# Attention in eight places of the array, a step that spans three pairs, and x folded into W0, in a fused four-layer kernel

## The reference

```python
x = x + _L0_cond_ref(x, W, A, Bm, scalings, idx0)  # x W^T + rank-16 adapter of 8: (x A_b^T) B_b^T s_b
x = x + _L1_cond_ref(x, idx1, w1)                  # einsum('bct,bcd->bdt'): mixes the 64 tokens, 1 of 200 matrices
x = x + _L2_cond_ref(x, cond, Wq, Wk, Wv, Wo)      # causal attention, 16 heads of 32, q scaled by min(cond, 4)
x = x + _L3_cond_ref(x, idx3, w3)                  # as layer 1, 1 of 8 matrices
```

## Time and profile before

| | |
|---|---|
| median of 3 runs | 714.54 us (713.11 to 714.82) |
| profiled execution | 714.74 us, span 713.2 us |
| mean granted TensorE clock | 0.988 |
| TensorE matmul rows | 683.2 us busy, 96% of the span |
| TensorE weight loads | 584.7 us, 82% |
| VectorE, ScalarE, GpSimd | 378.9, 319.9, 113.9 us |
| DMA | 31.68 MB, 44 GB/s over the span |

### The profile page before, as it was taken

The page is one execution under the profiler, slowest core; times in us unless marked ns, Lnnn a source line. Parts: engine busy times, 40 slices in busy tenths (PEclk is TensorE's granted clock), DMA queues, the critical chain, the costliest instruction groups (busy, mean ns, idle before and its releaser), DMA issues.

```text
span 713.2 us, 14872 instructions
## 1 busy us (share of the span) xinstructions
PE 683.2 (96%) x5240; PEld 584.7 (82%) x5240; DVE 378.9 (53%) x565; ACT 319.9 (45%) x648; POOL 113.9 (16%) x98
## 2 busy tenths in 40 slices
PE   5699999999999999999999999999999999999986
PEld 4489797888979798797979879797987979798774
DVE  3645555464555646455564645546463554636362
ACT  3544355443535544353554435354543535444342
POOL 4003012030301203030120303002030300303030
PEclk9979999999999999999999999999999999999998
DMA  6520111102011010201101020110202011020000
GB/s 185 191 94 8 53 37 35 49 4 81 7 52 37 33 52 4 81 7 52 37 30 54 5 81 7 52 37 18 65 5 81 7 52 37 9 75 4 29 1 30
DMA packets 32768, 31.68 MB, mean 44 GB/s; under 512 B 18550, under 2 KB 18550, under 8 KB 32758
## 3 DMA queue, kind: packets, MB, share of 16 engines
q1 hardware_dynamic: 32758, 31.55, 14.2%
HBM read 22.61 MB, written 8.91 MB: 44 GB/s over the span
## 4 chain that ended last, share of the span: by engine, by line
PE 92%; DMA 2%; DVE 2%; SPq 1%; issue 1%; ACT 0%; POOL 0%; ACTq 0%; DVEq 0%
PE banks L374 13%; PE banks L375 12%; PE banks L376 12%; PE banks L504 9%; PE banks L472 8%; PE banks L493 5%; PE banks L421 5%; PE banks L512 4%; PE banks L481 4%; PE banks L404 4%; PE banks L402 4%; PE banks L406 4%; PE banks L436 2%; PE banks L395 2%; PE banks L385 2%; PE banks L414 2%
## 5 line engine op out<-in xcount | busy, mean ns | idle before, releaser
L374 PE MATMUL banks<-x1T_hi,w_hi 128*128 128x256 f32 x512 | 148.3, 290 | 0.0
L375 PE MATMUL banks<-x1T_lo,w_hi 128*128 128x256 f32 x512 | 144.9, 283 | 0.0
L376 PE MATMUL banks<-x1T_hi,w_lo 128*128 128x256 f32 x512 | 144.8, 283 | 0.0
L374 PEld LDWEIGHTS banks<-x1T_hi,w_hi 128*128 128x128 f32 x512 | 98.1, 192 | 15.3 <-issue 15.3
L375 PEld LDWEIGHTS banks<-x1T_lo,w_hi 128*128 128x128 f32 x512 | 98.1, 192 | 0.0
L376 PEld LDWEIGHTS banks<-x1T_hi,w_lo 128*128 128x128 f32 x512 | 98.0, 191 | 0.0
L742 DVE COPY k_bd<-banks 32x512 f32<-32x512 f32 x64 | 44.2, 691 | 98.9 <-PE banks L376 98.2
L907 POOL TENSOR_TENSOR w_own<-w_in,own 128x128 f32<-128x128 f32 x32 | 14.7, 460 | 492.7 <-PE banks L421 287.0
L922 POOL TENSOR_TENSOR probs<-probs,row_max 128x1024 f32<-128x1024 f32 x32 | 61.0, 1907 | 84.2 <-DVE row_max L808 84.2
L677 ACT ACTIVATE probs<-probs 128x1024 f32<-128x1024 f32 x32 | 34.0, 1061 | 72.2 <-POOL probs L922 71.9
L802 DVE SCALAR_TENSOR_TENSOR probs<-banks,beta,mask 128x512 f32<-128x512 f32 x64 | 46.4, 747 | 37.2 <-PE banks L472 36.6
(11 more groups left out here) (93 smaller groups left out, 1222.5 us busy)
## 6 DMA issues: line engine op xcount, KB each, us to landing
x_in<-in_x_dram SPq DMA_DIRECT2D x16, 512.0 KB, 3.7
out_dram<-y SPq DMA_DIRECT2D x16, 512.0 KB, 2.8
b_sel<-b_parts SPq DMA_DIRECT2D x192, 32.0 KB, 1.8
w_in<-in_L_cond_weights_dram SPq DMA_DIRECT2D x128, 16.0 KB
probsT<-in_L_cond_W_dram SPq DMA_DIRECT2D x1, 1024.0 KB, 6.1
probs<-in_L_cond_Wk_dram SPq DMA_DIRECT2D x1, 1024.0 KB, 7.7
x_both<-in_L_cond_Wq_dram SPq DMA_DIRECT2D x1, 1024.0 KB, 10.0
probsT<-in_L_cond_Wv_dram SPq DMA_DIRECT2D x1, 1024.0 KB, 12.1
```

Source lines behind the costliest of these rows:

```text
L374: nc.tensor.matmul(out_ap, s_hi, m_hi, start=(k == 0), stop=False)
L375: nc.tensor.matmul(out_ap, s_hi, m_lo, start=False, stop=False)
L376: last = nc.tensor.matmul(out_ap, s_lo, m_hi, start=False, stop=(k == n - 1))
```

## The change

- **Attention in eight places.** q and k stay as the projections leave them (`qT`, `kT`, 32 rows per head), v too. A scores product is one head of one sequence: 32 rows, 64 columns, 64 streamed columns, 64 of them in a step. Consecutive ones go to the four row groups, then to the other column half; each row group has its own bank. An attention product is one head of one sequence too: 64 rows (tokens), 32 columns, again 64 in a step, over two row halves and four column quarters. Nothing is padded, so the placing copies go; ScalarE copies a half of k and all of v, VectorE the other half of k and q times beta, so that the mask is a plain addition.
- **Order.** Step i scores pair i, does the out projection and layer 3 of pair i-1, and takes pair i+1 from `adapters_down` to its values, and x of pair i+2 through `turn_x`. Step 0, twelve steps in a loop and three written out.
- **x in W0.** The identity is added to the transposed W0 on VectorE before the split, so `add_x` is a copy (one tile by ScalarE, one by VectorE).
- **Staging.** Each of the five matrices has a stage of its own, and all are loaded at once from ScalarE's DMA queue.
- `keep_x1` (the copy of x1 for layer 2's residual) moves from ScalarE to GpSimd; layer 2's output no longer shares `probs`.

The core of the diff:

```diff
-            def scores(i, t):
-                if t == 0:
-                    for placed in (k_placed_act, k_placed_dve, q_placed_act, q_placed_dve):
-                        pe.wait_ge(placed, i + 1)
-                for hp in range(HP):
-                    b = (5 + 2 * t + hp // 4) % 8
-                    last = nc.tensor.matmul(bank[b][:, hp % 4 * P:(hp % 4 + 1) * P], q_bd[:, t, hp, :],
-                                            k_bd[:, t, hp, :], start=True, stop=True)
...
+            def scores(i):
+                pe.wait_ge(k_copied_act, i + 1)
+                pe.wait_ge(k_copied_dve, i + 1)
+                pe.wait_ge(q_scaled, TILES * (i + 1))
+                for mm in range(NC // 2):
+                    for t in range(TILES):
+                        for r in range(SEQT):
+                            for h in range(2):
+                                for j in range(JG):
+                                    m, rows = 2 * mm + h, slice(j * HD, (j + 1) * HD)
+                                    last = nc.tensor.matmul(bank[SC[j]][half(h), key_columns(m, t, r)],
+                                                            qT[rows, m, own_tokens(t, r)],
+                                                            kT[rows, m, own_tokens(t, r)], start=True, stop=True)
+                last.then_inc(s_mm, 1)
...
+            def attend():
+                for t in range(TILES):
+                    for m in range(NC):
+                        for r in range(SEQT):
+                            for j in range(JG):
+                                at = j % 2 * BANK + (m // 2 * TILES + t) * P + m % 2 * S
+                                head = (JG * m + j) * HD
+                                last = nc.tensor.matmul(
+                                    attn_bank(r)[j * HD:(j + 1) * HD, m, t, :], v[half(r), t, head:head + HD],
+                                    probsT[half(r), j // 2, at:at + S], start=True, stop=True)
+                last.then_inc(av_mm, 1)
...
+            def step(i):
+                prev, nxt, nxt2 = after(i, -1), after(i, 1), after(i, 2)
+                scores(i)
+                if prev:
+                    for t in range(TILES):
+                        layer2_out(i - 1, t)
+                if nxt:
...
                     adapters_down(i + 1)
+                    layer0_dense()
+                    adapters_up(i + 1)
...
                 turn_probs(i, 0)
+                if prev:
+                    layer3()
...
                 turn_probs(i, 1)
+                if nxt:
+                    layer1()
...
+                attend()
+                if nxt:
+                    keys(i + 1)
...
+                    queries(i + 1)
+                    pe.wait_ge(attn_split, SEQT * (i + 1))
+                    values()
```

On VectorE:

```diff
-                    last = nc.vector.scalar_tensor_tensor(
-                        out=heads(probs[:, t, n * BANK:(n + 1) * BANK]), in0=heads(bank[(5 + 2 * t + n) % 8][:]),
-                        scalar=beta[:, bass.ds(i * TILES + t, 1)],
-                        in1=mask[:].unsqueeze(1).to_broadcast([P, HEADS // 2, S]), op0=ALU.mult, op1=ALU.add)
+                    last = nc.vector.tensor_tensor(
+                        heads(probs[:, g, n * BANK:(n + 1) * BANK]), heads(bank[SC[2 * g + n]]),
+                        mask[:].unsqueeze(1).to_broadcast([P, HEADS // 2, S]), ALU.add)
...
+            def step(i):
+                prev, nxt, nxt2 = after(i, -1), after(i, 1), after(i, 2)
+                for g in range(HG):
+                    mask_and_max(i, g)
+                    if prev:
+                        add_x1(i - 1, g)
                 sums(i, 0)
+                if nxt:
+                    sum_xa(i + 1)
+                    scale_xa(i + 1)
                 sums(i, 1)
+                if nxt:
                     xa_lo_part(i + 1)
+                    x0_copy(i + 1)
+                for g in range(HG):
+                    copy_pT(i, g)
+                if nxt:
+                    x1_copy(i + 1)
                     x1T_lo_part(i + 1)
```

More of the change, by code:

```diff
@@ new lines, in attn_bank, with in_chunks, in_steps, after @@
+        def attn_bank(r):
+            return bank[OUT[r]].rearrange("p (m t s) -> p m t s", m=NC, t=TILES)
+        def in_chunks(ap):
+            return ap.rearrange("p (c n) -> p c n", n=P)
+        block = ctx.enter_context(nc.Block())
+        LAST_ALIKE = PAIRS - 4
+        def in_steps(engine, step):
+            step(0)
+            with engine.Fori(1, LAST_ALIKE + 1) as i:
+                step(i)
+            for i in range(LAST_ALIKE + 1, PAIRS):
+                step(i)
+        def after(i, n):
+            return not isinstance(i, int) or 0 <= i + n < PAIRS
@@ new lines, in gather, with gather_b @@
+            def gather(dst, table, at, arrived, moved):
+                for n in range(PSEQ):
+                    t, b = divmod(n, SEQT)
+                    sp.dma_start(dst[half(b ^ t if moved else b), t, :],
+                                 table[bass.ds(at[n], 1), :, :].rearrange("a c e -> (a c) e")).then_inc(arrived, 16)
+            def gather_b(at):
+                for n in range(PSEQ):
+                    t, b = divmod(n, SEQT)
+                    for k, part in enumerate((0, 0, 1)):
+                        row = (k * SEQT + b) * RANK
+                        sp.dma_start(b_sel[row:row + RANK, t, :].bitcast(F32),
+                                     b_parts[part, bass.ds(at[n] * RANK, RANK), :]).then_inc(b_loaded, 16)
@@ new lines, in keys, with queries, values @@
+            def keys(i):
+                pe.wait_ge(x1_hi_done, TILES * (i + 1))
+                for m in range(NC):
+                    last = project_T(WK, MIX, m, split=TILES * (i + 1) if m == 0 else None)
+                    if m % 2 == 1:
+                        last.then_inc(k_mm, 1)
+            def queries(i):
+                for m in range(NC):
+                    last = project_T(WQ, SC, m)
+                    if m % 2 == 1:
+                        last.then_inc(q_mm, 1)
+            def values():
@@ L594, in _ @@
-            turn_matrix(4, groups_of(4)[0])
-            keys(0, range(NC))
-            pe.wait_ge(turned_lo, GROUPS)
-            with pe.Fori(0, PAIRS - 1) as i:
-                step(i)
-            step(PAIRS - 1, more=False)
+            turn_x1(0, 0)
+            turn_x1(0, 1)
+            keys(0)
+            pe.wait_ge(xT_split, TILES * 2)
+            queries(0)
+            turn_matrix(WO)
+            pe.wait_ge(turned_lo, GROUPS_OF[WV][-1] + 1)
+            values()
+            pe.wait_ge(turned_lo, GROUPS)
@@ L602, in _ @@
+            in_steps(pe, step)
+            for t in range(TILES):
+                layer2_out(PAIRS - 1, t)
+            layer3_ready(PAIRS - 1)
+            layer3()
         @block.scalar
@@ L631, in xa_hi_part @@
                 act.wait_ge(xa_hi_done, i + 1)
+                if not (isinstance(i, int) and i == 0):
+                    act.wait_ge(x0_mm, TILES * i)
                 n = SEQT * RANK
@@ L734, in _ @@
-            with act.Fori(0, PAIRS - 1) as i:
-                step(i)
-            step(PAIRS - 1, more=False)
+            copy_k(0)
+            take_matrix(WO)
+            copy_v(0)
+            in_steps(act, step)
+            copy_y(PAIRS - 1)
         @block.vector
@@ L886, in _ @@
             dve.wait_ge(tables_done, 1)
-            take_matrix(1)
+            take_matrix(WK)
             sum_xa(0)
             scale_xa(0)
-            take_matrix(2)
+            take_matrix(WQ)
             xa_lo_part(0)
-            take_matrix(3)
-            add_x(0)
+            x0_copy(0)
+            x_lo(1)
+            take_matrix(WV)
+            x1_copy(0)
             x1T_lo_part(0)
-            take_matrix(4)
-            dve.wait_ge(zeroed, 3)
-            with dve.Fori(0, PAIRS - 1) as i:
-                step(i)
-            step(PAIRS - 1, more=False)
+            copy_k(0)
+            scale_q(0)
+            take_matrix(WO)
+            in_steps(dve, step)
+            for t in range(TILES):
+                add_x1(PAIRS - 1, t)
         @block.gpsimd
```

811 lines of the change are left out of this document (386 added, 425 removed).

## The result

The changed kernel takes 727.86 us (725.0 to 729.35), the kernel before 714.68 beside it: 1.018 of the time, 95% interval 1.015 to 1.022. It is slower by 1.8%, where 685 us were forecast and 714 was the upper end of the range. The profiled run took 727.0 us, around a span of 725.3.

A forecast was written before the change was run, and what follows sets the result against it. TensorE was taken to bound the kernel (92% of the chain). Start-up 60, step 0 37.2, thirteen steps 516.1, step 14 38.9, end 31.2 and 1.5 outside gave 685 us; own range 673 to 700, overall 664 to 714.

The forecast's parts named there:

- The two blocks: Scores and attention products on TensorE: 128 records each over eight places, 1.32 us each, saving 2.17 and 1.18 us a step.
- In between: Record price between 7 and 30.4 ns: the mix's weight loads suggest up to 14 to 20 ns for four places.
- a place takes 60 ns a record: Scores and attention: each of eight overlapping places takes 60 ns per record, so 16 records take 0.96 us.
- records come no faster than now: Rival for scores and attention: feeding sets 30.4 ns a record, 92 us more, 777 us; chance 0.18 for anything above 15 ns.
- The new wait: TensorE before adapters up waits for VectorE's xa_lo_part, queued behind the softmax: 1.3 us a step, possibly 0.4 to 2.5.
- xa_sum and xa 0.42 each: Two terms of VectorE's chain before adapters up, 0.42 us each within a sum of 12.35 us, 13.0 with gaps.
- VectorE slowed while GpSimd works: Upper case for TensorE's wait before adapters up: 2.5 us a step instead of 1.3.
- a VectorE chain 1.6 us longer: Rival "part of it": this longer chain, or about 14 ns a record in scores and attention, gives 709 us; chance 0.14.
- The period: Ordinary step from scores to scores: 38.4 us without waits plus 1.3 of wait, 39.7 us.
- Step 0: First step, without layer 3 (1.1 us) and add_x1 (1.4 us) in its chain: 37.2 us.
- The start-up: Time before first scores: all matrices sent for at once, keys 3 us earlier at 41, first scores at 60 us, 54 to 66.
- The end: From the last step's first score to the finish, its softmax unhidden: 31.2 us.

The follow-up runs named there:

- e10_place: The changed kernel with score products reordered so that two in a row use the same 32 rows and 64 columns of the array: 732.02 us.
- e1_hold: The changed kernel with GpSimd's division of the first probabilities waiting until VectorE has written xa: 720.43 us, ratio 1.009.
- e12_late: The changed kernel with ScalarE issuing the loads of Wk, Wq, Wv and Wo only after A and Bm have landed: 720.56 us, ratio 1.011.
- e4_load: The changed kernel with weight loads back on SyncE's queue in the old order, and B's parts stored ahead of the w1 and w3 gathers: 715.67 us.
- e9_best: The changed kernel with old-order SyncE loads and stores, xa's sum in PSUM, later x0 copies, adapters up between first probability transposes and layer 3: 687.27 us.
- e6_pairs: The changed kernel with score products reordered so that consecutive ones use the same 32 rows and the two column halves: 727.34 us.
- e3_order: The changed kernel with adapters up moved behind the first probability transposes and layer 3, x0 copies behind the first pT copies: 705.84 us.

## Why the prediction was wrong

- **The two blocks.** Eight places do run side by side, as forecast; the price of a record was off. "In between" lay weight loads of up to 14 to 20 ns a record for four places, and I took the lower end, 7. Bursts of eight do start 6 to 7 ns apart, but four records of a mix don't show the gaps between bursts; the averages were 10.7 and 10.0. Each block was put at 1.32 us and cost 1.61 and 1.5: 0.29 + 0.19 a step. That a place takes 60 ns a record, which the sum took for the limit, is not borne out either: e10_place repeats a place 32 times, at 60 ns that alone would add 1.9 us, and it added 0.40. The rival "records come no faster than now", at 0.18, did not happen, nor did the Trainium skill's limit of about 25 ns between starts (TensorE: Matmul & The Clock Gate, "Wait — 56ns, not 53.3ns?"), which these rows contradict for small products in different places, at 10.7 and 10.0 ns.
- **The new wait.** This is the step that failed inside the loop. Its place and its releaser were named; its size was not: 1.3 us forecast, 1.82 measured. TensorE's arrival was right (T + 12.4 by the rows, 12.2 forecast, T the last record's start). VectorE's sum counted "xa_sum and xa 0.42 each" from rows in which GpSimd rested, and "VectorE slowed while GpSimd works" stood only as an upper bound of 2.5. The product alone took 1.57 more. Without it the sum would have been too long: VectorE ended at T + 14.1 (255.42 - 241.35), 0.7 later than the 13.4 forecast, so that the other pieces took 0.9 less. The prediction did have a rival with this mechanism, a VectorE chain 1.6 us longer, at 709 and a chance of 0.14. The Trainium skill has the rule that was left out (SBUF — State Buffer, "Who interferes with whom"): a VectorE instruction with two SBUF inputs contends with a GpSimd instruction that reads SBUF, and the one that comes second stands until the first has finished. This case's traces agree, at 0.417 against 1.99 us for VectorE in second place and 1.04 against 2.03 us for GpSimd (e1_hold).
- **The period** was 40.67 for 39.7. 0.29 + 0.19 for the blocks and 0.52 for the wait give 1.00, the whole of it (the forecast is 39.67 before rounding). Over thirteen steps that is 12.6 us.
- **Step 0** was put at 37.2, a step less layer 3 and VectorE's additions. It took 41.3. Adapters up came at T + 13.1 (91.04 - 77.92) where 13.5 less two additions, 12.1, were counted, after 4.75 us of idle; the product took 1.95 us here too. Right behind that idle the granted clock was 0.57 from 91 to 95 us, which is some 1.7 us of work lost, and the attention product stood for 1.03 us in its middle, which the profile puts down to no releaser. With the blocks' 0.5 this is about the 4.1.
- **The start-up** is the largest miss, 16.6 us: "I put the keys 3 us earlier, at 41". They came at 56.27. This is the step that failed ahead of the loop. The text named the stores that share the engines with what is still on the way, and counted a gain all the same. It didn't follow Bm, whose four transfers are issued in 14.6 us instead of 6.12 while all 5 MB are in flight, nor what SyncE issues behind it, the gathers of w1 and w3 ahead of B's parts among it. e12_late shows the first (7.9 us back), e4_load both together (12.8 back). The 3.8 that remain were forecast too low in any case: the keys of e4_load stand at 43.48, not 41, and from keys to first scores it takes 20.3 us, in e4_load and in the change, where 19 were counted.
- **The end** was put at 31.2 and took 34.9. The probabilities were divided when forecast (T + 12.5). The splits were done 1.5 us later than T + 18.1, behind transposes at a granted clock of 0.50 (702.33 to 705.70). The out projection then began at full clock, and from 712.6 to 716.0 the granted clock was 0.50 again. Timeline of TensorE at the end of the changed kernel:

```profile
711.41 0.50 PE L518 MATMUL banks<-w_hi,attnT_hi 128*128 128x512 f32 x1 [2.01 <-DVE attnT_lo L762]
...
712.75 0.63 PE L520 MATMUL banks<-w_lo,attnT_hi 128*128 128x512 f32 x1
...
719.76 1.21 PE L412 MATMUL banks<-x_y,w_own 64*64 64x512 f32 x8 [0.94 <-DVE x_y L848]
```

  8.35 us from the first of these products to the mix, where 6.35 were counted, after idle times of 4.59, 0.88 and 2.01 us in the fourteen before.
- **The sum**: 16.6 for the start-up, 12.6 for the period, 4.1 for step 0, 3.2 for two long steps, 1.7 for step 14 and 3.7 for the end are 41.9, of the 42.0 between the forecast and the profiled run's 727.0. The cost of the array was forecast well enough. e9_best, with the same blocks in the array, comes to 687.27, but only once the wait and the loads have been put elsewhere, and that it lies near 685 is luck: its first scores are 4.6 us later than forecast, its step 0 is 4.3 longer and its end 3.7, and thirteen steps without the wait, 38.92 each, take back 10.1.

## What to carry to other kernels

When a step is reordered, look up for each VectorE instruction of the new chain whether both its inputs are in SBUF and what GpSimd does at that moment; the duration from the old trace holds only for the old neighbours. Then ask where the consumer of the chain stands: moving it behind 2.0 us of other work brought as much as taking the stretches away. Loads that are all "sent for at once" can delay the one that is needed first, and with it all that the same queue issues behind it; whether that one's small size made it worse was not tested. In such a queue, put first what the next engine in the chain waits for.

## What the runs showed of the hardware

- Eight places of the array take small fp32 records every 10.0 to 10.7 ns on average over 128; bursts of eight start 6 to 7 ns apart, with gaps up to 60 ns. A product that follows one in the same place adds 12.5 ns (0.40 us for 32).
- Between a VectorE instruction with both inputs in SBUF and a GpSimd instruction on SBUF, the one that began first kept its time (VectorE's division 1.25 us, GpSimd's division 1.90) and the other was stretched (GpSimd's copy 1.04 to 2.03, VectorE's product 0.417 to 1.99).
- A VectorE instruction that is held by GpSimd goes on almost at once: the product ended 0.28 us after GpSimd's division, less than its own 0.417. The ends of GpSimd's rows are rough, so this rests on some tenths.
- In the change, e4_load, e12_late and e6_pairs two steps out of fifteen took 42.3 us, six steps apart; in the change the granted clock in one of them was 0.51 from 337.0 to 340.5, right after the wait before adapters up. All four have a period of 40.67 to 40.70. None of the runs with a shorter period (38.91 to 40.22) had such a step, not even e3_order with its slow product; e10_place, at 41.08, had one, the second. Why the clock falls in one step and not in the five before, after the same wait, stays open. Together the two are 3.2 us.
